# Attention stage of a two-layer block: normalising on ScalarE, a product as two 64-row tiles, gate logits by 32-column tiles

## The reference

```
# layer 0 (16 states per batch), as far as it matters here
x  = x + (H @ Wo.T + bo) * sigmoid(xn @ Wg.T + bg) ... * silu(ffn(xn))
# layer 1
xn = (x - mean(x)) / sqrt(var(x) + 1e-5)
q, k, v = xn @ Wq.T + bq, xn @ Wk.T + bk, xn @ Wv.T + bv   # 16 heads of 16
scores  = einsum('ibhd,jbhd->ijbh', q, k) / 4              # i, j: the batches; causal
attn    = exp(s - max) / (1 + sum(exp(s - max)))
logits  = xn @ wg                                          # 8 experts, top 2
x = x + (attn @ v) * silu(moe(xn, logits))
```

## Time and profile before

| | us |
|---|---|
| median of 3 runs (1622.37 to 1627.42) | 1622.44 |
| the profiled execution, its own time | 1624.57 |
| its span in the trace | 1622.6 |
| `attend` in it, from about | 334.8 to 671.8 |
| VectorE busy from 335 to 660 | 285.65 of 325 |
| TensorE busy from 335 to 660 | 280.06 of 325 |

### The profile page before, as it was taken

The page is one execution under the profiler, slowest core; times in us unless marked ns, Lnnn a source line. Parts: engine busy times, 40 slices in busy tenths (PEclk is TensorE's granted clock), DMA queues, the critical chain, the costliest instruction groups (busy, mean ns, idle before and its releaser), DMA issues. The chain is left out here.

```text
span 1622.6 us, 23549 instructions
## 1 busy us (share of the span) xinstructions
PE 1318.7 (81%) x7615; PEld 903.2 (56%) x7615; DVE 1061.7 (65%) x1979; ACT 643.9 (40%) x947; POOL 610.5 (38%) x572
## 2 busy tenths in 40 slices
PE   2999997769999898145599999999999999999300
PEld 2666664347777777011267666667566666667200
DVE  3677773047999999699755655555655556555297
ACT  1444453213222222045444555354544445543263
POOL 2112220003666666434333333333344333343245
PEclk9999998669999999555599999999999999999755
DMA  8000004500000000100121313131222213122496
GB/s 286 1 0 0 0 0 178 237 26 27 26 26 26 26 26 26 52 0 0 58 72 47 103 42 109 50 92 51 73 75 77 72 51 98 50 99 50 111 321 219
DMA packets 70758, 116.84 MB, mean 72 GB/s; under 512 B 6449, under 2 KB 57523, under 8 KB 68496
## 3 DMA queue, kind: packets, MB, share of 16 engines
q1 hardware_dynamic: 51456, 74.38, 13.4%
q0 software_dynamic: 12720, 33.96, 6.8%
q10 hardware_dynamic: 6496, 7.36, 1.4%
HBM read 66.13 MB, written 50.33 MB: 72 GB/s over the span
## 5 line engine op out<-in xcount | busy, mean ns | idle before, releaser
L1578 ACT ACTIVATE e_h_all<-e_pH,e_b1c,e_h_scale 128x512 f32<-128x512 f32 x256 | 199.8, 780 | 369.0 <-PE e_pH L1625 365.3
L1644 PE MATMUL e_pY<-e_w_hi,e_h_hi 128*128 128x256 f16 x1024 | 279.3, 273 | 5.2 <-DVE e_w_lo L1489 5.2
L1646 PE MATMUL e_pY<-e_w_hi,e_h_lo 128*128 128x256 f16 x1024 | 279.1, 273 | 0.0
L1645 PE MATMUL e_pY<-e_w_lo,e_h_hi 128*128 128x256 f16 x1024 | 279.1, 273 | 0.0
L1404 POOL DMA_INDIRECT e_xg<-xn_rows,e_icol x136 | 154.0, 1132 | 297.1 <-DVE e_icol L1430 255.4
L1517 DVE TENSOR_TENSOR e_h_lo<-e_h_all,e_h_hi 128x512 f16<-128x512 f32 x256 | 177.3, 693 | 105.2 <-ACT e_h_hi L1578 92.6
L1623 PE MATMUL e_pH<-e_x_hi,e_w_hi 128*128 128x512 f16 x512 | 195.7, 382 | 9.8 <-issue 6.0
L1625 PE MATMUL e_pH<-e_x_hi,e_w_lo 128*128 128x512 f16 x512 | 195.8, 382 | 0.0
L1624 PE MATMUL e_pH<-e_x_lo,e_w_hi 128*128 128x512 f16 x512 | 195.8, 382 | 0.0
L1416 POOL DMA_INDIRECT expert_rows<-e_yo,e_dcol x128 | 130.8, 1022 | 154.9 <-DVE e_yo L1541 123.9
L1541 DVE SCALAR_TENSOR_TENSOR e_yo<-e_pY,e_y_scale,logit_st 128x1024 f32<-128x1024 f32 x32 | 41.1, 1284 | 157.4 <-PE e_pY L1646 152.3
(11 more groups left out here) (231 smaller groups left out, 2547.0 us busy)
## 6 DMA issues: line engine op xcount, KB each, us to landing
raw<-expert_w SPq DMA_DIRECT2D x18, 1024.0 KB
expert_rows<-r_zero SPq DMA_DIRECT2D x16, 1024.0 KB, 16.2
xn_rows<-c_xn SPq DMA_DIRECT2D x16, 512.0 KB, 2.9
f_ya<-expert_rows SPq DMA_DIRECT2D x16, 512.0 KB, 5.1
f_yb<-expert_rows SPq DMA_DIRECT2D x16, 512.0 KB, 6.0
out<-f_ya SPq DMA_DIRECT2D x16, 512.0 KB, 3.5
x_st<-x ACTq DMA_DIRECT2D x4, 1536.0 KB, 13.9
e_xg<-xn_rows,e_icol POOLq DMA_INDIRECT x136
```

Of the source, the lines that this page charges most:

```text
L1578: last = act.activation(dst, pH[h % NPH][:, :], ACT.Relu, bias=b1c[eu][:, h:h + 1], scale=h_scale[eu][:, 0:1])
L1644: pe.matmul(pY[:, q, :], h_hi[:, h, cols], w2_hi[:, h, :], start=(h == 0), stop=False)
L1645: pe.matmul(pY[:, q, :], h_hi[:, h, cols], w2_lo[:, h, :], start=False, stop=False)
L1646: last = pe.matmul(pY[:, q, :], h_lo[:, h, cols], w2_hi[:, h, :], start=False, stop=(h == HT - 1))
```

## The change

1. `normalise` moves from VectorE to ScalarE. VectorE subtracted the mean and multiplied by the scale; ScalarE computes scale times x plus a bias. GpSimd works out that bias, minus mean times scale, with two more operations per tile, and `r1` and the new `nmr` have two buffers. On ScalarE `normalise(t+2)` stands between `states(t+3)` and the exponential of tile t.
2. `output` multiplies rows 0 to 63 for the first two batches and rows 64 to 127 for the other two, in place of 128 rows for both.
3. The logits are computed turned over: the gate weights, padded to 32 columns, are the stationary side and 128 columns of activations move. Each batch has 32 rows of `pL`. ScalarE copies that out (`take_logits`), TensorE transposes it (after V, ahead of `turn`), and ScalarE copies the result to `logit_st` (`put_logits`, right after the exponential of the same tile). The padding lengthens each row of `late` by 48 numbers.
4. `den` and `rden` share the buffer of `mx`. Some statistics wait for a semaphore of GpSimd.

```diff
@@ -825,18 +831,24 @@
             @block.gpsimd
             def _(pool):
                 pool.sem_inc(pv_step, PV + 1)
-                for n, (t, value) in enumerate(((mhalf[:, :], -0.5), (eps[:, :], EPS))):
+                for n, (t, value) in enumerate(((mhalf[:, :], -0.5), (eps[:, :], EPS), (mone[:, :], -1.0))):
                     pool.memset(t, value).then_inc(open_, 1)
                     pool.wait_ge(open_, n + 1)
 
-                def scale(t):
+                def scale(t, u, reused=True):
                     pool.wait_ge(stats, t + 1)
                     pool.tensor_tensor(ta[:, :], mv[:, :, 1], eps[:, :], ALU.add).then_inc(rchain, 1)
-                    pool.wait_ge(rchain, t + 1)
-                    pool.tensor_tensor(r1[:, :], ta[:, :], mhalf[:, :], ALU.pow).then_inc(r_ready, 1)
+                    pool.tensor_tensor(tb[:, :], mv[:, :, 0], mone[:, :], ALU.mult).then_inc(rchain, 1)
+                    pool.wait_ge(rchain, 3 * t + 2)
+                    if reused:
+                        pool.wait_ge(xn_ready, t - 1)
+                        pool.sem_inc(passed, 1)
+                    pool.tensor_tensor(r1[u][:, :], ta[:, :], mhalf[:, :], ALU.pow).then_inc(rchain, 1)
+                    pool.wait_ge(rchain, 3 * t + 3)
+                    pool.tensor_tensor(nmr[u][:, :], tb[:, :], r1[u][:, :], ALU.mult).then_inc(r_ready, 1)
 
                 for t in range(3):
-                    scale(t)
+                    scale(t, t % 2, reused=t >= 2)
 
                 def body(i, u, left):
                     t = 2 * i + u
@@ -861,7 +873,7 @@
                             pool.tensor_tensor(o, o, part, ALU.add).then_inc(pv_step, 1)
                             n += 1
                         if j == 1 and left >= 3:
-                            scale(t + 3)
+                            scale(t + 3, 1 - u)
 
                 tiles(pool, body)
 
@@ -882,21 +894,15 @@
                         last = dve.bn_stats(st[:, b, :], v.x_st[:, t, b * D:(b + 1) * D])
                     last.then_inc(bn, 1)
                     dve.wait_ge(bn, t + 1)
+                    if not (isinstance(t, int) and t == 0):
+                        dve.sem_inc(passed, 1)
+                        dve.wait_ge(r_ready, t)
                     dve.sem_inc(passed, 1)
                     for b in range(B):
                         last = dve.bn_aggr(mv[:, b, :], st[:, b, :])
                     last.then_inc(stats, 1)
 
-                def normalise(t, u, stores):
-                    dve.wait_ge(r_ready, t + 1)
-                    dve.wait_ge(xn_out[u], 16 * stores + 16)
-                    for b in range(B):
-                        last = dve.tensor_scalar(xn[u][:, b, :], v.x_st[:, t, b * D:(b + 1) * D],
-                                                 mv[:, b, 0:1], r1[:, b:b + 1], ALU.subtract, ALU.mult)
-                    last.then_inc(xn_ready, 1)
-
                 layer0(0)
-                normalise(0, 0, 0)
 
                 flat = v.bqkv
                 dve.memset(bias3[:, :], 0.0).then_inc(masked, 1)
@@ -915,7 +921,6 @@
                 last.then_inc(bias_ready, 1)
                 dve.wait_ge(bias_ready, 6)
                 layer0(1)
-                normalise(1, 1, 0)
 
                 def body(i, u, left):
                     t = 2 * i + u
@@ -928,8 +933,6 @@
                         last = dve.tensor_tensor(qk[:, PAIR0[j]:PAIR0[j] + w, :], q[:, j:B, :],
                                                  spread(k[u][:, j, :], w), ALU.mult)
                     last.then_inc(sm, 1)
-                    if left >= 2:
-                        normalise(t + 2, u, i + 1)
                     dve.wait_ge(sm, SM * t + 1)
                     for j in range(B):
                         w = B - j
@@ -945,23 +948,23 @@
                                       sc[:, :, :, :].rearrange("p j i h -> p j (i h)"), spread(mx[:, :], B),
                                       ALU.subtract).then_inc(ex_in, 1)
                     dve.wait_ge(ex_out, t + 1)
-                    dve.tensor_reduce(den[:, :], ex[:, :, :, :].rearrange("p j i h -> p (i h) j"), AX.X,
+                    dve.tensor_reduce(mx[:, :], ex[:, :, :, :].rearrange("p j i h -> p (i h) j"), AX.X,
                                       ALU.add).then_inc(sm, 1)
                     dve.wait_ge(sm, SM * t + 4)
-                    dve.tensor_scalar(den[:, :], den[:, :], 1.0, None, ALU.add).then_inc(sm, 1)
+                    dve.tensor_scalar(mx[:, :], mx[:, :], 1.0, None, ALU.add).then_inc(sm, 1)
                     dve.wait_ge(sm, SM * t + 5)
-                    dve.reciprocal(rden[:, :], den[:, :]).then_inc(sm, 1)
+                    dve.reciprocal(mx[:, :], mx[:, :]).then_inc(sm, 1)
                     dve.wait_ge(sm, SM * t + SM)
                     dve.wait_ge(pv_step, steps_through(t - 2))
                     dve.tensor_tensor(att[u][:, :, :, :].rearrange("p j i h -> p j (i h)"),
-                                      ex[:, :, :, :].rearrange("p j i h -> p j (i h)"), spread(rden[:, :], B),
+                                      ex[:, :, :, :].rearrange("p j i h -> p j (i h)"), spread(mx[:, :], B),
                                       ALU.mult).then_inc(att_ready, 1)
 
                 tiles(dve, body)
 
             @block.scalar
             def _(act):
-                for s in (l_evac, v_evac):
+                for s in (v_evac,):
                     act.sem_inc(s, 1)
 
                 def states(t, u, reused=True):
@@ -972,6 +975,28 @@
                     act.activation(hs[u][:, :, :], v.h_st[:, :, bass.ts(t, CPT)].rearrange("p l c -> p c l"),
                                    ACT.Copy).then_inc(hs_ready, 1)
 
+                def normalise(t, u, stores):
+                    act.wait_ge(r_ready, t + 1)
+                    act.sem_inc(passed, 1)
+                    act.wait_ge(xn_out[u], 16 * stores + 16)
+                    act.sem_inc(passed, 1)
+                    for b in range(B):
+                        last = act.activation(xn[u][:, b, :], v.x_st[:, t, b * D:(b + 1) * D], ACT.Identity,
+                                              scale=r1[u][:, b:b + 1], bias=nmr[u][:, b:b + 1])
+                    last.then_inc(xn_ready, 1)
+
+                def take_logits(t):
+                    act.wait_ge(l_done, t + 1)
+                    act.sem_inc(passed, 1)
+                    act.activation(lgT[:, :], pL[:, 0:P], ACT.Copy).then_inc(l_taken, 1)
+
+                def put_logits(t):
+                    act.wait_ge(l_turned, t + 1)
+                    act.sem_inc(passed, 1)
+                    act.activation(v.logit_st[:, :, t, :],
+                                   pL[:, P:2 * P].rearrange("p (b e) -> p b e", e=GRP)[:, :, 0:E],
+                                   ACT.Copy).then_inc(l_evac, 1)
+
                 def take(dst, src, done, evac, t, scale=1.0):
                     act.wait_ge(done, t + 1)
                     act.activation(dst[:, :, :], src[:, :, :], ACT.Copy, scale=scale).then_inc(evac, 1)
@@ -986,16 +1011,15 @@
                     if reused:
                         act.wait_ge(pv_step, steps_through(t - 2))
                     take(vv[u], pY, v_done, v_evac, t)
-                    act.wait_ge(l_done, t + 1)
-                    act.sem_inc(passed, 1)
-                    act.activation(v.logit_st[:, :, t, :], pL[:, 0:B * E].rearrange("p (b e) -> p b e", e=E),
-                                   ACT.Copy).then_inc(l_evac, 1)
 
                 states(0, 0, reused=False)
                 states(1, 1, reused=False)
+                normalise(0, 0, 0)
                 take(xnT, pT, t_done, t_evac, 0)
                 states(2, 0)
+                normalise(1, 1, 0)
                 take_qk(0, 0, reused=False)
+                take_logits(0)
                 take_v(0, 0, reused=False)
                 take(xnT, pT, t_done, t_evac, 1)
                 take_qk(1, 1)
@@ -1004,9 +1028,13 @@
                     t = 2 * i + u
                     if left >= 3:
                         states(t + 3, 1 - u)
+                    if left >= 2:
+                        normalise(t + 2, u, i + 1)
                     act.wait_ge(ex_in, t + 1)
                     act.activation(ex[:, :, :, :], ex[:, :, :, :], ACT.Exp).then_inc(ex_out, 1)
+                    put_logits(t)
                     if left >= 1:
+                        take_logits(t + 1)
                         take_v(t + 1, 1 - u)
                     if left >= 2:
                         take(xnT, pT, t_done, t_evac, t + 2)
@@ -1019,9 +1047,10 @@
                 def output(t, u):
                     pe.wait_ge(hs_ready, t + 1)
                     for n in range(2):
+                        half = slice(2 * GRP * n, 2 * GRP * n + 2 * GRP)
                         last = pe.matmul(pX[:, 2 * n:2 * n + 2, :].rearrange("p b d -> p (b d)"),
-                                         hs[u][:, :, :].rearrange("p c l -> p (c l)"),
```

(33 more changed lines are left out.)

## The result

The changed kernel takes 1662.45 us (median of 4 runs, 1659.44 to 1667.01), the kernel before in the same comparison 1624.1: a ratio of 1.0236, interval 1.0205 to 1.0267. It is slower by 38 us. The forecast was 1661, range 1634 to 1686. The profiled execution took 1667.01 us, its span is 1665.2.

A forecast was written before the change was run, and what follows sets the result against it. VectorE set the pace before; the new waits would bind the tiles in a ring of 11.9 + 8.1 + 1.5 = 21.5 us against 19.0. Thirteen periods +38.0, start -2.9, end +3.6: net +38.7, forecast 1661 us, range 1634 to 1686.

The forecast's parts named there:

- The ring: Logits wait for the previous tile's exponential, VectorE's product multiply for the output behind them: period 21.5 us against 19.0.
- Rival F: VectorE stays the only bound, 14.2 us of work per tile: 1583 us, if X to S falls under 6.6; chance 0.05.
- S to X: From VectorE's product multiply (S) to the exponential (X): 11.9 us, 13.0 in tiles with a table load.
- X to S: From a tile's exponential to VectorE's next product multiply: 8.1 us at full clock, bounds 7.05 and 9.4.
- rival B: Matmuls on different array tiles run wholly side by side with no drain: 1647 us; chance 0.15.
- the 5.4 us for the loads: ScalarE's table load ahead of the states costs 1.07 us more in five of the 13 periods: 5.4 us.
- the clock term: TensorE's clock falls after its pause ahead of the logits, in nearly all tiles: 1.5 us per tile.
- rival C: TensorE's clock holds through the pause ahead of the logits: 21 us less, 1640 us; chance 0.12.
- Thirteen periods: From the exponential of tile 0 to that of tile 13: 279.5 + 5.4 - 246.9 = +38.0 us.
- Start: Up to the exponential of tile 0: product Q 1.8 us earlier, logits and output shorter, transpose added: -2.9 us.
- End: From the exponential of tile 13 to that of tile 14, behind take_qk(15): 17.9 against 14.34 us, +3.6.

The follow-up runs named there:

- the filler run: The changed kernel with ten more f32 products per tile, written to an unread bank, in TensorE's pause ahead of the logits: 1635.9 us.
- the first experiment: The changed kernel with the transpose of a tile's logits put one tile later, into a PSUM bank of its own: 1590.95 us, ratio 0.9791.
- the last experiment: The kernel of the first experiment with ScalarE's loop body begun ahead of take_qk with a 128x4 copy, to move the table load: 1587.31 us.

## Why the prediction was right, by its own steps

**The ring** stands as described, and the signs that were named are in the profile: VectorE stands 6.6 and 7.4 us ahead of its product multiply (5 to 7 forecast), TensorE 4.9 and 6.0 ahead of the logits, released by ScalarE's copy, and layer0 and q times k take 4.68 and 3.00. Cutting it at one place gives 71 us back, and adding it alone to the kernel before costs 74. Rival F, in which VectorE sets the pace, is near what the whole change does once the ring is cut: not at 1583 but at 1587 to 1594. F had 14.2 us of work for VectorE because it took layer0 and q times k from the first body, where no large GpSimd operation runs beside them; the periods without the ring are 16.45 to 16.92. F's threshold is also summed wrongly: 18.3 less the 11.9 of S to X leaves 6.4 for X to S, not 6.6. Nothing else hangs on it.

**S to X.** Forecast 11.9 and 13.0 us, measured 12.20 and 13.26. ScalarE's four take 2.07 where 1.7 was put, and beside GpSimd VectorE's subtraction takes 0.79, not 0.42; 0.2 had been put for that. GpSimd's longer chain was hidden as said (ready at S + 8.5).

**X to S.** The products were put too high and the clock too low. At full clock, in the changed kernel's first tile:

```profile
346.38 2.08 ACT L984 ACTIVATE c_xn<-x_st,c_nmr,c_r 128x256 f32<-128x256 f32 x4 [8.74 <-POOL c_nmr L848]
...
351.60 1.04 PE L1090 MATMUL c_pY<-c_bias,c_ones 128*128 128x512 bf16 x2 [1.12 <-ACT c_xnT L1002]
...
362.15 0.65 PE L1084 MATMUL c_pL<-c_xnT,late 128*32 128x128 f32 x16
...
362.72 0.61 PE L1090 MATMUL c_pY<-c_bias,c_ones 128*128 128x512 bf16 x2
...
367.70 1.13 PE L1051 MATMUL c_pX<-late,c_hs 64*128 64x512 f32 x4
...
369.00 1.23 DVE L887 TENSOR_TENSOR prod_st<-c_pX,prod_st 128x1024 f32 x1 [14.96 <-PE c_pX L1051]
...
382.26 0.41 ACT L1034 ACTIVATE c_ex<-c_ex 128x256 f32<-128x256 f32 x1
```

The logits take 362.72 - 362.15 = 0.57 us where 1.0 was put, and output's start to S takes 369.00 - 367.70 = 1.30 against 370.83 - 368.78 = 2.05 before, so 0.75 saved and not 0.43. X to S at full clock is then 0.56 + 0.57 + (369.00 - 362.72) = 7.41, not 8.1; the filler run has the same 7.41. The rule that in f32 only the second record of one product and the first of the next can run together was wrong: four column tiles run nearly together (0.57 us; by V's rows 0.43 is an estimate for together and 1.72 for in a row), and two row tiles save 0.75 of at most 0.86.

The kernel before could have told this. "The trace has no matmul on part of the array" is a misreading: `mix` has 256 f32 records with 64 columns of weights, for rows 0 to 63 and 64 to 127 of one output in turn. In the kernel before:

```profile
100.71 0.64 PE L606 MATMUL a_pGU<-a_low,dsum 128*64 128x512 f32 x1
100.72 0.64 PE L608 MATMUL a_pGU<-a_high,dsum 128*64 128x512 f32 x1
101.19 0.59 PE L606 MATMUL a_pGU<-a_low,dsum 128*64 128x512 f32 x1
```

Two tiles start 0.01 us apart and the next pair about 0.43 to 0.48 later, which is what a single full record of 512 columns takes in the earlier trace rows (1.72 for four). So there were rows for rival B, tiles wholly side by side, and against the rule that was used. The Trainium skill, "TensorE: Matmul & The Clock Gate", Part 3, has matmuls on different tiles start a few ns apart. The rows above agree (0.01 us). The drain at a change of tiling mode, of which the Trainium skill, "TensorEngine Tiling (Array Packing)", Key Properties, speaks, is small here. From K's first product to the logits it is 362.15 - 358.60 = 3.55 us, where it was 362.33 - 358.87 = 3.46 before; so at most 0.09 us for the switch into the tiles, and 0.14 (0.57 less 0.43) for the one out of them.

The clock took 9.84 - 7.41 = 2.43 and 9.05 - 7.41 = 1.64 us of the two turns, 2.0 in the mean as the filler shows, where 1.5 was put. The turn that costs more is the one behind a table load. There TensorE stood 5.99 us and not 4.92 before the logits, and V took 5.91 and not 5.18. So the 1.06 us more on ScalarE come with 0.8 more on TensorE; the 5.4 us for the loads had only the first. That the longer pause makes the slow stretch longer is read from the rows of these turns and not tested by itself.

The evidence for the clock term was also misread. The fall is in seven of thirteen tiles of the kernel before, not absent from most, so rival C had less for it than was said.

That 8.1 + 1.5 = 9.6 came near the measured (9.84 + 9.05)/2 = 9.45 is luck: 0.7 us too much for the products stood against 0.5 too little for the clock.

**Thirteen periods** came to 285.42 - 246.93 = +38.5 us, forecast +38.0. The mechanism was forecast; that the sum is off by half a microsecond is luck, since per tile 0.3 too little in S to X and 0.5 too little for the clock met 0.7 too much for the products.

**Start.** Forecast -2.9, measured 382.26 - 383.89 = -1.6. Q(0) starts at 351.60 and not 350.3, as the normalising of tile 0 starts at 346.38 and takes 2.08, where 0.9 us in all had been put for the longer path. From Q(0) to S(0) the products gave 0.3 more than put, and S(0) to X(0) took 0.2 more.

**End.** Forecast +3.6, measured (685.20 - 667.68) - 14.34 = +3.2, by the cause that was named: the exponential of tile 14 follows the copy of k of tile 15 directly.

```profile
667.68 0.42 ACT L1034 ACTIVATE c_ex<-c_ex 128x256 f32<-128x256 f32 x1 [0.47 <-DVE c_ex L947]
...
684.27 1.02 ACT L1002 ACTIVATE c_k<-c_pX 128x1024 f32<-128x1024 f32 x1 [2.79 <-PE c_pX L1094]
685.20 0.41 ACT L1034 ACTIVATE c_ex<-c_ex 128x256 f32<-128x256 f32 x1
```

The exponential of tile 15 is 40.4 us later than before. The spans of the two profiled executions differ by 42.6 us, the medians by 38.4; the 2.2 us between stage and span lie outside these tiles and within what single executions differ by.

Rival C, the clock holding through the pause, is refuted by the rows and by the filler. B was nearly right on the products (0.75 us a tile of its 1.0) and wrong on the time, since the clock took more than was put.

## What to carry to other kernels

Before counting what an edit takes from the busiest engine, walk each new wait once around: which instruction gives it, what stands ahead of that in its engine's program, and what is queued behind the wait. If the walk comes back to where it began within one tile, its sum is the new period, whatever the busy shares say. A value that is taken out, turned and taken out again should come back a tile later, in a bank of its own; that turned +2.4% into -2.1% here. And a pause of TensorE ahead of work on such a ring can be paid twice, since the work behind it may start at the lower clock: here it took 2.0 us a tile. Before putting that a trace has no row for something, look in its other stages as well.

## What was not expected of the hardware

In f32, eight products with 32-column weights and 128 moving columns took 0.57 us at full clock in four column tiles, a third of the 1.72 that one after the other would take by V's rows (an estimate), and two 64-row products of 512 columns 1.13 against 1.88, with tiling switched and back in each tile. TensorE kept its higher clock through pauses of 1.7 to 1.9 us in the first experiment (1.00 from 400 to 580 us) and of up to 1.7 us in the filler run (1.00), and lost it in each turn of the ring, after pauses of 4.6 to 6.0 us. In the kernel before, a pause of about 1.0 us behind the eight-column logits was followed by the lower clock in seven tiles and not in others. ScalarE's 128x256 operation with scale and bias from memory takes 0.59 us, and four of them 2.07, so one follows the other at about 0.49. In all of these kernels the table load of 1.28 us stands at ScalarE's first operation of the loop body; the last experiment moved the one and the other went with it.
